# Attention over 32 graphs: one weighing of the values for all heads, softmax shares spread on GpSimd and transposed by TensorE, and a new slot plan

## The reference

```
q, k, v = x Wq^T + bq, x Wk^T + bk, x Wv^T + bv          (split into 8 heads)
scores  = (q k^T) * D^-0.5 * (adj + adj)                 per head, 256 x 256
attn    = softmax(scores, axis=-1)
ctx     = attn v                                         heads side by side again
out     = layernorm(x + ctx Wo^T + bo)
```

## Time and profile before

| | |
|---|---|
| median of 3 runs | 515.63 us (514.15 to 516.78) |
| the profiled execution, its own time | 513.55 us |
| its span | 511.7 us |
| busy share of the span | PE 91%, PEld 77%, DVE 84%, ACT 75%, POOL 69% |
| mean granted TensorE clock | 0.984 of full speed |

### The profile page before, as it was taken

One profiled execution on the slowest core, in us unless ns is written; L12 is line 12 of the kernel. 1 busy time (PEld: TensorE's weight loads), 2 busy tenths in 40 slices (PEclk: granted clock), 3 DMA queues, 4 the chain that ended last, 5 costly groups with the idle time before them and its releaser, 6 DMA issues.

```text
span 511.7 us, 15227 instructions
## 1 busy us (share of the span) xinstructions
PE 467.9 (91%) x4742; PEld 392.1 (77%) x4742; DVE 428.9 (84%) x1815; ACT 382.2 (75%) x1257; POOL 351.3 (69%) x518
## 2 busy tenths in 40 slices
PE   4649999999999999999999999999999999998962
PEld 3438888888888888888888888888888888877751
DVE  5548899888888998888888898888889988889972
ACT  2379888787878878787888878787878878777750
POOL 4724748787776768687676778777676778764445
PEclk9859999999999999999999999999999999999998
DMA  5809897979789897979799797979799697895201
GB/s 164 205 0 215 198 263 184 233 206 238 194 225 240 188 266 180 236 195 234 208 231 247 178 255 181 241 192 237 209 224 266 167 241 194 195 233 115 63 21 63
DMA packets 40322, 100.11 MB, mean 196 GB/s; under 512 B 9649, under 2 KB 17842, under 8 KB 40242
## 3 DMA queue, kind: packets, MB, share of 16 engines
q1 hardware_dynamic: 26930, 73.96, 59.0%
q10 hardware_dynamic: 13312, 25.17, 17.4%
HBM read 26.22 MB, written 8.39 MB: 68 GB/s over the span
## 4 chain that ended last, share of the span: by engine, by line
PE 73%; DVE 15%; issue 7%; POOL 2%; ACT 2%; DMA 1%; DVEq 0%; POOLq 0%; SPq 0%; ACTq 0%
PE turn_bank L223 18%; PE ctx_bank L278 11%; PE row_bank L211 9%; PE out_bank L290 9%; PE proj_bank L240 9%; PE v_bank L253 9%; PE ctx_bank L266 7%; DVE probs L341 5%; DVE y L373 4%; DVE context L366 2%; DVE low_top L349 2%; ACT stack L145 1%; PE row_bank L240 1%; DVE shares L361 1%; DMA turned_probs<-in_wk 1%
## 5 line engine op out<-in xcount | busy, mean ns | idle before, releaser
L447 ACT ACTIVATE probs<-probs,low_top 128x256 f32<-128x256 f32 x512 | 256.1, 501 | 92.7 <-DVE low_top L349 90.3
L356 DVE COPY turned_probs<-turn_bank 128x512 f32<-128x512 f32 x224 | 154.8, 691 | 53.7 <-PE turn_bank L223 53.4
L341 DVE CUSTOM_DVE_ANT_0 probs<-row_bank,adj_rows 128x256 f32<-128x256 f32 x512 | 193.2, 416 | 6.5 <-PE row_bank L211 6.4
L223 PE MATMUL turn_bank<-ident,probs 128*128 128x128 f32 x1024 | 157.2, 276 | 1.0 <-DVE turned_probs L356 1.0
L223 PEld LDWEIGHTS turn_bank<-ident,probs 128*128 128x128 f32 x1024 | 119.5, 141 | 43.4 <-ACT probs L447 20.8
L211 PE MATMUL row_bank<-stack 128*128 128x256 f32 x512 | 124.3, 325 | 4.0 <-DVE top L341 4.0
L240 PE MATMUL proj_bank<-xt_parts,w_parts 128*128 128x512 f32 x360 | 105.3, 401 | 11.6 <-ACT whole L477 7.5
L447 ACT ACTIVATION_READ_ACCUMULATOR probs<-probs,low_top 128x1 f32 x512 | 96.0, 188 | 0.0
L540 POOL TENSOR_TENSOR parts<-whole,parts 128x512 fp32r<-128x512 f32 x64 | 83.0, 1297 | 5.1
L211 PEld LDWEIGHTS row_bank<-stack 128*128 128x128 f32 x512 | 78.3, 193 | 6.0 <-DVE top L341 5.5
L538 POOL CAST parts<-whole 128x512 fp32r<-128x512 f32 x64 | 39.3, 614 | 54.8 <-ACT whole L477 53.2
(11 more groups left out here) (44 smaller groups left out, 470.6 us busy)
## 6 DMA issues: line engine op xcount, KB each, us to landing
stack<-parts SPq DMA_DIRECT2D x492, 128.0 KB, 3.1
xt<-in_x_t SPq DMA_DIRECT2D x16, 512.0 KB, 4.0
adj_rows<-in_adj ACTq DMA_DIRECT2D x16, 512.0 KB, 5.2
xr<-in_x ACTq DMA_DIRECT2D x16, 512.0 KB, 7.6
out<-result ACTq DMA_DIRECT2D x32, 256.0 KB, 4.3
turned_probs<-in_wk SPq DMA_DIRECT2D x1, 256.0 KB, 3.7
turned_probs<-in_wq SPq DMA_DIRECT2D x1, 256.0 KB, 3.6
turned_probs<-in_wv SPq DMA_DIRECT2D x1, 256.0 KB, 3.8
```

Source lines behind the costliest of these rows:

```text
L223: last = nc.tensor.transpose(turn_bank[o % 2][:, c * S + t * P:c * S + (t + 1) * P], probs[:, o % RING, t * S + c * P:t * S + (c + 1) * P] ...
L341: last = nc.vector.tensor_tensor_reduce(probs[:, o % RING, t * S:(t + 1) * S], row_bank[o % 2][:, t * S:(t + 1) * S], adj_rows[:, (n // 2) ...
L356: nc.vector.tensor_copy(turned_probs[:, o, :], turn_bank[o % 2][:]).then_inc(moved_dve, 1)
L447: last = nc.scalar.activation(tile, tile, ACT.Exp, bias=low_top[:, n % 2, o, t:t + 1], accum_out=sums[:, n % 2, o, t:t + 1])
```

## The change

- `turned_probs` has twelve places instead of eight; head o of graph g goes to place (8 g + o) mod 12. A move waits for the weighing of the graph that had the place before.
- Heads 0 and 4 are moved by ACT, not only head 4.
- `weigh_v` runs once per graph, for all eight heads, with 32 instructions (as many as before in two visits) in slot 1 of the next step, into the whole of `ctx_bank`.
- The shares: DVE `divide` takes all 16 reciprocals of a partition at once (slot 6). POOL `spread_shares` (new, first in slot 7) copies them to `wide`, each 32 times (128x512). PE `turn_shares` (slot 2 of the next step) transposes `wide` with four full 128x128 transposes into `inv_bank`, a bank of its own. The 16-instruction column-tiled version is gone.
- `copy_inverse` (ACT slot 3), `scale_context` (DVE slot 4) and `cut_context` (POOL slot 4) run once per graph on 128x512 instead of twice on 128x256.
- `project_v` goes two graphs ahead (slot 4, read by ACT in slot 5) and shares `out_bank` with `project_out`, which moves from slot 6 to slot 7. `add_residual` moves to slot 0 of the following step, the statistics to slots 1 and 2, `aggregate` to slot 3, `add_bias` to slot 2 one graph later.
- The key and query projections, their reads and cuts, and the cuts of the features get other slots. In both the even and the odd steps there is now a `read_kq` and a `cut_kq` in slot 4 and in slot 7.

```diff
-KQ_SLOTS = {(0, 7): (0, 0), (1, 0): (0, 1), (1, 3): (1, 0), (1, 4): (1, 1),
-            (1, 7): (2, 0), (0, 0): (2, 1), (0, 3): (3, 0), (0, 4): (3, 1)}
-KQ_CUT_SLOTS = {(1, 1): 0, (1, 5): 1, (0, 1): 2, (0, 5): 3}
-X_SLOTS = {(0, 4): 0, (0, 5): 1}
-ON_ACT = (4,)
+TURNED = 12
+KQ_SLOTS = {(0, 5): (0, 0), (0, 6): (0, 1), (1, 0): (1, 0), (1, 3): (1, 1),
+            (1, 5): (2, 0), (1, 6): (2, 1), (0, 0): (3, 0), (0, 3): (3, 1)}
+KQ_CUT_SLOTS = {(0, 7): 0, (1, 4): 1, (1, 7): 2, (0, 4): 3}
+X_SLOTS = {(0, 1): 0, (0, 2): 1}
+ON_ACT = (0, 4)
...
+            def turn_shares(g):
+                pe.wait_ge(widened, g + 1)
+                wait(pe, inverted, g)
+                for half_ in range(2):
+                    for t in range(T):
+                        last = nc.tensor.transpose(inv_bank[:, half_ * S + t * P:half_ * S + (t + 1) * P],
+                                                   wide[:, t, J * half_:J * (half_ + 1), :].rearrange("p h d -> p (h d)"),
+                                                   ident[:])
+                last.then_inc(inv_made, 1)
...
             def project_out(g):
-                pe.wait_ge(ctx_low, 2 * g + 2)
+                pe.wait_ge(ctx_low, g + 1)
+                pe.wait_ge(v_ready, min(g + 4, B))
                 wait(pe, y_ready, g)
...
                     if o == 1 and is_graph(g - 1):
-                        turn_shares(g - 1, 1)
-                        weigh_v(g - 1, 1)
-                    if o == 2 and is_graph(g + 1):
-                        project_v(g + 1)
-                    if o == 5 and is_graph(g):
-                        turn_shares(g, 0)
-                        weigh_v(g, 0)
-                    if o == 6 and is_graph(g - 1):
+                        weigh_v(g - 1)
+                    if o == 2 and is_graph(g - 1):
+                        turn_shares(g - 1)
+                    if o == 4 and is_graph(g + 2):
+                        project_v(g + 2)
+                    if o == 7 and is_graph(g - 1):
                         project_out(g - 1)
...
+            def spread_shares(g):
+                pool.wait_ge(shares_ready, g + 1)
+                wait(pool, inv_made, g)
+                nc.gpsimd.tensor_copy(wide[:].rearrange("p t h d -> p (t h) d"),
+                                      shares[:].rearrange("p t h -> p (t h)").unsqueeze(2).to_broadcast([P, T * H, D])
+                                      ).then_inc(widened, 1)
...
                 for o in range(H):
+                    if o == 7 and is_graph(g):
+                        spread_shares(g)
                     if (g % 2, o) in X_SLOTS and is_pair(g + 4):
                         low_x((g + 4) // 2, X_SLOTS[g % 2, o])
                     if (g % 2, o) in KQ_CUT_SLOTS:
-                        ahead = kq_ahead(g, o, KQ_CUT_SLOTS)
+                        ahead = kq_ahead(g, o)
                         if is_pair(g + ahead):
                             cut_kq((g + ahead) // 2, KQ_CUT_SLOTS[g % 2, o])
-                    if o == 0 and is_graph(g - 1):
-                        cut_context(g - 1, 0)
-                    if o == 3 and is_graph(g - 1):
-                        cut_context(g - 1, 1)
+                    if o == 4 and is_graph(g - 1):
+                        cut_context(g - 1)
```

More of the change, by code:

```diff
@@ L66, in build @@
         low_top = sb("low_top", [P, 2, H, T])
-        sums = sb("sums", [P, 2, H, T])
-        shares = sb("shares", [P, 2, H, T])
+        sums = sb("sums", [P, 2, T, H])
+        shares = sb("shares", [P, T, H])
         probs = sb("probs", [P, RING, T * S])
-        turned_probs = sb("turned_probs", [P, H, T * S])
-        inverse = sb("inverse", [P, S])
-        context = sb("context", [P, 2, S])
+        turned_probs = sb("turned_probs", [P, TURNED, T * S])
+        wide = sb("wide", [P, T, H, D])
+        inverse = sb("inverse", [P, 2 * S])
+        context = sb("context", [P, 2 * S])
         ctx_parts = sb("ctx_parts", [P, 2, 2, 2, S], F32R)
@@ L156, in is_pair, with kq_ahead @@
             return 0 <= g // 2 < PAIRS
[L158 to L162, removed]
+        def kq_ahead(g, o):
+            return 3 if g % 2 else 4 if o >= 5 else 2
         block = ctx.enter_context(nc.Block())
@@ L257, in project_v @@
                 last.then_inc(v_made, 1)
[L259 to L268, removed]
@@ new lines, in weigh_v @@
+            def weigh_v(g):
+                pe.wait_ge(v_ready, g + 1)
+                wait(pe, ctx_ready, g)
+                for o in (H - 1, *ON_ACT):
+                    wait_moved(pe, g, o)
+                for half_ in range(2):
+                    for t in range(T):
+                        for o in range(J * half_, J * half_ + J):
+                            c = D * (o % J)
+                            last = nc.tensor.matmul(ctx_bank[c:c + D, half_ * S:(half_ + 1) * S],
+                                                    v[:, (g // 2) % 2, g % 2, t, o * D:(o + 1) * D],
+                                                    turned_probs[:, (H * g + o) % TURNED, t * S:(t + 1) * S], start=(t == 0),
+                                                    stop=(t == T - 1), tile_position=(0, c), skip_group_check=True)
@@ L353, in move_turned, with divide, scale_context @@
                 dve.wait_ge(turned, 8 * g + o + 1)
[L355 to L367, removed]
+                wait(dve, ctx_made, (H * g + o - TURNED) // H + 1)
+                nc.vector.tensor_copy(turned_probs[:, (H * g + o) % TURNED, :], turn_bank[o % 2][:]).then_inc(moved_dve, 1)
+            def divide(g):
+                dve.wait_ge(probs_ready, H * g + H)
+                wait(dve, widened, g)
+                nc.vector.reciprocal(shares[:], sums[:, g % 2]).then_inc(shares_ready, 1)
+            def scale_context(g):
+                dve.wait_ge(ctx_made, g + 1)
+                dve.wait_ge(inverted, g + 1)
+                wait(dve, ctx_low, g)
+                nc.vector.tensor_tensor(context[:], ctx_bank[:], inverse[:], ALU.mult).then_inc(ctx_ready, 1)
             def add_residual(g):
@@ L547, in low_x, with cut_context @@
                                         ALU.subtract).then_inc(xt_low, 1)
-            def cut_context(g, half_):
-                pool.wait_ge(ctx_ready, 2 * g + half_ + 1)
+            def spread_shares(g):
[4 more added lines that the diff above has]
+                                      ).then_inc(widened, 1)
+            def cut_context(g):
+                high, low = (ctx_parts[:, g % 2, n].rearrange("p f s -> p (f s)") for n in range(2))
+                pool.wait_ge(ctx_ready, g + 1)
                 wait(pool, out_made, g - 1)
[L552 to L555, removed]
+                nc.gpsimd.tensor_copy(high, context[:]).then_inc(ctx_high, 1)
+                pool.wait_ge(ctx_high, g + 1)
+                nc.gpsimd.tensor_tensor(low, context[:], high.bitcast(F32), ALU.subtract).then_inc(ctx_low, 1)
             def add_bias(pair, b):
```

78 lines of the change are left out of this document (32 added, 46 removed).

## The result

The changed kernel takes 522.98 us (median of 4 runs, 522.61 to 523.65). The kernel before took 516.17 in the same comparison. The ratio is 1.014, with a 95% interval of 1.011 to 1.017: slower by 1.4%. The forecast was 518 (range 499 to 531), with slower as the likeliest sign. So the direction and the mechanism held, and the size did not: the forecast change was +2.3 us, or +0.45%, which the prediction itself put within what can't be told from no change, and the measured one is +6.8 us.

The account below looks back on a forecast made before the run. PE bounds the kernel before; changed, a loop through POOL's queue does: 14.73 us a step against 14.53. 28 steps +5.6, steps 29 and 30 -3.8, start 0, end +0.5: +2.3, 515.9 us as profiled, 518 median, range 499 to 531.

Parts of the forecast that it names:

- The bound of the kernel before: PE bounds the steady step: its terms plus a 0.27 us wait for DVE's reciprocals make 14.53 us.
- PE's saving: On PE, share instructions, one visit and the 0.27 us wait go: 13.43 us a step, 1.10 less.
- The other sums: Work per step after the change: DVE 11.9 us, ACT at most 12.1, POOL with 1.77 us of room in even steps.
- The loop: From PE's turning of head 2 through DVE, ACT and POOL's queue to project_out and back: 9.32 + 5.41 = 14.73 us.
- The key projection of slot 5: On PE, it waits up to 0.1 us for ACT's read_kq of slot 4, hidden in the later wait.
- Steps 29 and 30: Last steps, without cut_kq: DVE bounds them at 12.0 us each instead of 13.9, together -3.8 us.
- The start: Before the first step: graph 1's values add about 1.4 us, the first step is shorter by the same, total 0.
- The end: After the last steps: a longer chain against a visit missing in the last step, +0.5 us.
- The full gain: The wait before project_out doesn't form, PE bounds at 13.43 us a step: 481 us; 12 in 100.
- rival 2: The loop's chain is shorter by 0.4 to 0.9 us: 493 to 507 us; 13 in 100.
- rival 3: Slower: the spread on POOL takes 3.5 us (533 us), or the loop's links stretch by 0.4 (529 us); together 13 in 100.
- rival 4: PE's idling of 1.3 us in each step lowers the granted clock: time beyond 540 us; 2 in 100.

Follow-up runs that it names:

- both orders: Changed kernel with POOL cutting the context ahead of the keys and ACT reading the keys ahead of its move: 483.07 us, ratio 0.939 to the kernel before.
- the kernel in which ACT reads first: Changed kernel with ACT's reads of keys or queries put ahead of its move of head 0 or 4: 508.76 us, ratio 0.988 to the kernel before.
- POOL's order changed: Changed kernel with POOL's slot 4 cutting the context ahead of the keys, nothing else: 487.23 us, ratio 0.947 to the kernel before.

## Why the prediction was right, and where its sizes were off

**The bound of the kernel before** was read rightly: PE's terms and the wait for DVE's reciprocals. Removing the wait alone gave 0.31 us a step. The busy share of PE in the steady part was forecast to fall to about 91%, and it fell to 281.38/300 = 94%. PE's own way is 0.3 us a step longer than forecast (14.85 - 1.12 = 13.73 against 13.43), and the profile shows 0.2 us less of waiting (18.6 us in 20 times) than the starts do.

**PE's saving.** Forecast 13.43 us a step if nothing else held it; 13.49 measured with both orders changed. The four transposes were the largest error of a term, 0.43 (265.04 to 265.47) for a guess of 0.35. The price of a visit, 0.26 by the terms, was measured as 0.28.

**The other sums.** DVE is busy for 12.3 us of a step (249.11 of 300), 0.4 more than the forecast 11.9, and still has room: 0.6 us more for it changed nothing. ACT has 11.9, where at most 12.1 was forecast. POOL was forecast to have 1.77 us of room in even steps; it waits 1.88 us there, and 1.36 us more work changed nothing. The spread takes 0.61, as the one-operand row said. What the prediction drew from the Trainium skill (GPSIMD Engine Reference, section 3.1), that one-input loops take less for an element than two-input ones, agrees with the trace: 0.61 for the spread against 1.28 to 1.30 for a subtraction of the same size.

**The loop.** By the profile's own chain of work, the way from the turning behind the visit through DVE, ACT and POOL to the output projection and back is the one that ended last, as forecast. The forecast chain of thirteen links was off by 0.01 us in 9.32. PE's part of the loop was forecast as 5.41 and is 5.52 (273.64 to 279.16): the output projection after a wait takes 1.52 to the next start, not the 1.43 of a pipelined one, and the single visit 1.87, not 1.83. So the step is 14.85 and not 14.73, and the first term of the sum is 28 x 0.32 = +9.0 in place of +5.6. (The measured +9.5 also holds +0.9 for step 28, told below, and -0.2 for step 1, which takes 14.63.) That is the term that was mis-sized most, by 3.4 us; the start (2.4) and the end (1.1) are the others. The wait itself was forecast as 1.30; by starts it is 273.64 - 272.20 - 0.32 = 1.12, since PE's own way is longer by 0.2: 0.08 for the transposes and 0.15 in slot 5, where the wait for ACT's read was put at up to 0.1, less 0.04 in the other slots.

**The key projection of slot 5** was said to be hidden. It is, in the changed kernel. Once the larger wait was gone it cost 0.17 us a step, 4.2 us between the two medians.

**Steps 29 and 30.** -3.8 forecast, -3.84 measured, at 12.0 us a step: without a cut of keys the loop falls away, and DVE is busy for 22.78 of the 23.97 us.

**The start.** Forecast 0, measured +2.4. The count of work moved ahead was incomplete: besides the values of one more graph, one more half of a key piece (0.7) is projected before the visit of step 1. PE comes out of its long wait in the start 0.51 us later (33.07 against 32.56). From there on its list up to that visit holds one value projection more (36.22 to 38.26, so 2.04, at the lower clock for much of it, not 1.43), one half more (0.70), one visit less (1.58), and PE waits 0.46, 0.64 and 0.27 for ACT's reads where it waited 0.44 and 0.27 for DVE. That is 0.51 + 2.04 + 0.70 - 1.58 + 0.66 = +2.3. But the starts scatter: in the other kernels with the changed slot plan the visit of step 1 lies at 53.47 to 54.53, against 54.76 here, and in the kernel before with two moves on ACT at 53.56, against 52.38. So of this +2.4 an unknown part, about 1 us by these numbers, may be scatter between executions. The account fits these two profiles, and making the exponentials earlier didn't help; taking the work itself out of the start wasn't tried.

**The end.** +0.5 forecast, +1.6 measured. The last output projection takes 2.56 us in place of 1.70 (below), 0.9 of it.

**The rivals.** The full gain (481 us, 12 in 100) didn't come in the changed kernel. It is what the kernel with both orders gives, 483.07, by its own condition: the wait in front of the output projection gone. What stood against it, the order of POOL's queue, was what decided. The shorter chain (rival 2) and the stretched one (the second half of rival 3) are both refuted by the trace, 9.33 us for 9.32. The spread on POOL as a cost is refuted by the copy made three times. The clock (rival 4) didn't fall in the steady part, although PE waited in each step; it fell in two places behind it, which are told below. The three chances given for the sign (0.33, 0.23, 0.44) are those of the cases added up only roughly: the cases give 0.34, 0.21 and 0.45.

## What to carry to other kernels

When engines work through fixed queues, sum each engine's work, but then follow one turn of the loop from a late producer to its consumer and add what stands ahead of each link in its queue: here the sums said 7% faster, the loop said slower, and the order of two blocks in one queue was nearly the whole difference. Of the two pieces in the same slot here, the one whose operands came earlier and whose consumer was the bounding engine had to go first. And price a part in the schedule that it will run in: the second move on ACT is worth 1.8% in the kernel before and nothing in the changed one.

## What the runs showed that wasn't expected

PE's waits of 1.1 us in every step left the granted clock at 1.00 from 100 to 400 us. In step 28, which has no key projections in slots 5 and 6 but still a cut of keys in slot 4, the same wait grew to 1.94 us, and the clock was lower behind it. The timeline of PE and the busy times of two stretches there, in the changed kernel:

```profile
466.66 2.14 PE L298 MATMUL out_bank<-w_parts,ctx_parts 128*128 128x256 f32 x12 [1.94 <-POOL ctx_parts L566]
468.59 1.05 PE L224 MATMUL turn_bank<-ident,probs 128*128 128x128 f32 x4
```

```profile
464.00:469.00 5.00, 3.06 (x20) 2.76 (x19) 3.28 (x17) 3.19 (x13) 4.47 (x9) 0.87 0.67 146
469.00:472.00 3.00, 3.00 (x28) 2.59 (x30) 2.30 (x9) 1.82 (x6) 2.23 (x3) 0.65 0.94 210
```

Four turnings took 1.05 us and not 0.60, as at the lower level of 1.2 GHz. From this output projection to the visit it is 4.56 us (466.66 to 471.22). In the steady step the same work takes 273.64 to 277.29, less 0.69 for the key projection of slot 0 that is missing here: 2.96. So the lower clock cost 1.60 us, and with the missing projection the step is 15.73 us and not 14.85. The kernel in which ACT reads first shows the same in its step 28 (15.21 against 14.37), behind a wait of only 1.46 us. With POOL's order changed that step has no such wait and takes 11.95. At the end of the changed kernel, behind a wait of 3.48 us, the last output projection runs at a lower clock as well:

```profile
511.58 2.56 PE L298 MATMUL out_bank<-w_parts,ctx_parts 128*128 128x256 f32 x12 [3.48 <-POOL ctx_parts L566]
```

It took 1.70 us in the kernel before, behind a wait of 2.22 us:

```profile
502.71 1.70 PE L290 MATMUL out_bank<-w_parts,ctx_parts 128*128 128x256 f32 x12 [2.22 <-POOL ctx_parts L554]
```

And in the kernel in which ACT reads first it took 1.71 us behind a wait as long as that of the changed kernel:

```profile
498.34 1.71 PE L298 MATMUL out_bank<-w_parts,ctx_parts 128*128 128x256 f32 x12 [3.48 <-POOL ctx_parts L566]
```

So the length of the wait just before alone doesn't tell what the clock will do. What does is not shown by these runs.
